# A graph-attention kernel: TensorE gets four unread products at each of its five waits of a slot, and two PSUM banks hold two uses each

## The reference, cut to what matters

```python
x = x + _L0_gnn_ref(_layernorm(x), edge_index, ...)      # attention, 4 heads
x = x + _L0_ffn_ref(_layernorm(x)[None], ...)[0]         # 6 experts, top 2
x = x + _L1_gnn_ref(_layernorm(x), edge_attr_64, ...)    # attention, 1 head
x = x + _L1_ffn_ref(_layernorm(x)[None], ...)[0]         # 8 experts, all
# inside an attention:
e = leaky_relu(a_src[src] + a_dst[dst])
m = segment_max(e, dst); e = exp(e - m[dst])
out = segment_sum(e / segment_sum(e, dst)[dst] * h[src], dst)
```

## Time and profile before

| | us |
|---|---|
| median of 3 runs | 5728.6 |
| lowest and highest | 5703.49 and 5729.56 |
| the profiled execution's own time | 5700.18 |
| its span, first to last instruction | 5698.1 |
| first attention, steady part, 50 slots from 336.1 to 1848.6 | 1512.5, 30.9 a slot |
| second attention, steady part, 50 slots from 2926.2 to 4378.7 | 1452.5, 29.6 a slot |

### The profile page before, as it was taken

The page is one execution under the profiler, slowest core; times in us unless marked ns, Lnnn a source line. Parts: engine busy times, 40 slices in busy tenths (PEclk is TensorE's granted clock), DMA queues, the critical chain, the costliest instruction groups (busy, mean ns, idle before and its releaser), DMA issues. The chain is left out here.

```text
span 5698.1 us, 88959 instructions
## 1 busy us (share of the span) xinstructions
PE 4033.3 (71%) x21808; PEld 3026.7 (53%) x21809; DVE 2571.1 (45%) x8219; ACT 1553.1 (27%) x4325; POOL 2144.2 (38%) x2095
## 2 busy tenths in 40 slices
PE   5176666676667777884356666666666699999999
PEld 3144444444444456773234444444444488888888
DVE  7255555555555677555333343333433451222111
ACT  2122222222222221331222222222222233333333
POOL 0455555555555402327555555555555200000000
PEclk9565666655665556996666666666666699999999
DMA  3222222222222322443333333323223400000000
GB/s 98 70 73 69 70 71 70 72 68 70 71 68 72 53 85 80 163 141 102 91 74 75 73 71 72 72 72 74 71 70 71 81 6 7 5 5 5 5 5 8
DMA packets 382428, 367.94 MB, mean 65 GB/s; under 512 B 249324, under 2 KB 309388, under 8 KB 382242
## 3 DMA queue, kind: packets, MB, share of 16 engines
q0 software_dynamic: 107072, 272.84, 18.7%
q1 hardware_dynamic: 272774, 92.39, 6.7%
q10 hardware_dynamic: 2396, 0.84, 0.1%
HBM read 324.13 MB, written 41.59 MB: 64 GB/s over the span
## 5 line engine op out<-in xcount | busy, mean ns | idle before, releaser
L681 POOL DMA_INDIRECT g_G<-rows,g_pack x1856 | 1895.8, 1021 | 1793.9 <-PE bank L714 1105.5
L714 PE MATMUL bank<-g_G,g_MB 128*125 128x260 f32 x1856 | 833.7, 616 | 418.8 <-DVE acc L921 379.7
L714 PE MATMUL bank<-g_G,g_M 128*125 128x257 f32 x1856 | 760.5, 572 | 419.6 <-DVE acc L921 404.0
L714 PEld LDWEIGHTS bank<-g_G,g_MB 128*125 128x125 f32 x1856 | 529.8, 304 | 639.7 <-DVE acc L921 362.9
L714 PEld LDWEIGHTS bank<-g_G,g_M 128*125 128x125 f32 x1856 | 497.1, 285 | 608.5 <-DVE acc L921 414.4
L921 DVE SCALAR_TENSOR_TENSOR acc<-acc,g_c,bank 125x65 f32 (+1 forms) x2320 | 623.9, 319 | 220.3 <-PE bank L714 150.7
L1363 DVE SCALAR_TENSOR_TENSOR X<-bank,e_cw,X 125x256 f32 (+1 forms) x400 | 175.2, 480 | 844.9 <-PE bank L1189 844.9
L1259 ACT ACTIVATE e_h<-bank,e_bi_c,e_sc_c 128x250 f32<-128x250 f32 x800 | 403.6, 555 | 559.4 <-PE bank L1180 421.6
L1023 DVE TENSOR_SCALAR g_gone<-bank 125x64 f32<-125x64 f32 (+1 forms) x116 | 23.2, 200 | 1129.6 <-remote 1076.6
L787 ACT ACTIVATE g_mt_d<-bank,unode 125x256 bf16<-125x256 f32 x928 | 384.1, 464 | 521.0 <-PE bank L699 492.4
L863 ACT ACTIVATE g_c<-g_delta 125x32 f32<-125x32 f32 (+1 forms) x116 | 25.4, 219 | 1592.1 <-DVE g_delta L1061 1534.1
(11 more groups left out here) (300 smaller groups left out, 4608.4 us busy)
## 6 DMA issues: line engine op xcount, KB each, us to landing
g_G<-rows,g_pack POOLq DMA_INDIRECT x1856
acc<-in_edge_attr SPq DMA_DIRECT2D x50, 531.2 KB
g_pack<-edge_pack SPq DMA_DIRECT2D x928, 2.0 KB
g_drow<-edge_dst SPq DMA_DIRECT2D x928, 1.0 KB
expert_out<-x_y SPq DMA_DIRECT2D x54, 256.0 KB
g_qe<-edge_q SPq DMA_DIRECT2D x464, 1.0 KB
rows<-acc SPq DMA_DIRECT2D x25, 253.9 KB
rows<-n_T SPq DMA_DIRECT2D x25, 251.0 KB
```

The source lines that it names most:

```text
L681: nc.gpsimd.indirect_dma_start(G[:, r, q, :], None, rows_d[l], bass.IndirectOffsetOnAxis(ap=pack[:, r, q, 0:1], axis=0)).then_inc(S(p + f" ...
L714: mm_ = nc.tensor.matmul(bank[4 + u % 2][0:TN, 0:HW], left, G[:, rk, q, :], start=(c == 0), stop=(c == C - 1))
```

## The change

`busy()` issues four bf16 products of 128 x 128 by 128 x 512 into bank 7. Their operands are the constant table `iota_b`, and nothing reads their result. It has no wait and counts up nothing. It is called ahead of five waits in TensorE's order: ahead of the row turn, ahead of the selection turn, ahead of `sums(2, 0)`, ahead of the products for the maxima, and ahead of those at L766. To make bank 7 free, `selT_ps` moves into bank 0 beside `rowT_ps`, and `Xe_ps` moves into bank 6 beside `V_ps`. No wait or count of a semaphore changes.

```diff
+WARM = 4
...
-            selT_ps = bank[1][:, 0:2 * QH]
+            selT_ps = bank[0][:, 2 * P:2 * P + 2 * QH]
...
-            Xe_ps = bank[7][:, 0:KM * QH]
+            Xe_ps = bank[6][:, 2 * P:2 * P + KM * QH]
...
+                    def busy():
+
+                        for _ in range(WARM):
+                            nc.tensor.matmul(bank[7][:, :], iota_b[:, :], iota_b[:, :].unsqueeze(1).broadcast_to([P, 4, P]), start=True, stop=True)
+
                     def slot(i, r, t):
...
+                        busy()
                         if one:
                             if l == 0:
                                 pe.wait_ge(S(p + f"rows_in{r1}"), filled(t, r, 1, 16 * Q))
...
                         sums(3, U - 1)
+                        busy()
                         if one:
 
                             pe.wait_ge(S(p + "SEL"), i)
...
+                        busy()
                         sums(2, 0)
                         sums(2, 1)
...
                         sums(2, 3)
+                        busy()
                         if one:
 
                             pe.wait_ge(S(p + "MB"), i * V)
...
                         sums(2, 5)
+                        busy()
                         if one:
 
                             pe.wait_ge(S(p + "rhs"), i)
```

## The result

The changed kernel takes 5866.1 us (median of 4 runs, 5847.0 to 5879.0), the one before 5716.2 us beside it (4 runs, 5703.5 to 5729.6). The ratio is 1.026, with an interval of 1.024 to 1.029: slower by 150 us. The forecast, 5873, was 7 us off. As will be seen, that is in part luck: two terms of its sum were wrong in opposite directions.

The account below looks back on a forecast made before the run. GpSimd's gathers and its two waits were taken to set the slot. Over 58 slots each, 2.0 us (first attention) and 0.5 (second) gave 116 + 29 = 145; 5700.18 + 145 = 5845, plus 28 to the median: 5873, range 5640 to 6080.

Parts of the forecast that it names:

- Call 1: Ahead of the row turn, wholly in wait A and on the path: adds 1.7 us a slot at the low clock.
- wait A: GpSimd's idle 3.09 us a slot, ended by `sums(3, 6)`; said to grow to 4.5 to 5 us.
- wait B: GpSimd's idle 6.10 us a slot, until VectorE's L1023 and `sums(2, 4)`; expected to change by nothing.
- Calls 2 and 3: Around the selection turn, where a gather has no reserve: 0.7 us a slot, ends -0.6 and +2.9.
- Calls 4 and 5: Ahead of L754 and L766: up to 1.7 us each, hidden by 3.8 us of cover and 2.58 us idle; nothing.
- The credit for the clock in the second attention: A higher clock shortens the second attention's slot: 1.2 us credited beyond call 1's 1.7, leaving +0.5 a slot.
- 1.6 us after the last gather: In the first attention, L1023 starts 1.6 us after GpSimd's last gather, though V's products were recorded as ended earlier.
- if wait A doesn't grow: Sign of being wrong: it would mean that the clock was already up when call 1 began.
- the clock pays: Rival: high clock from call 1 on, slots 1.3 and 1.9 us shorter, 5543 us; 0.23 together with a between case, 5671.
- It cancels: Rival: the second attention gains what the first loses, 5700 to 5757 us; chance 0.13.
- the clock doesn't rise: Rival: every call paid at the low clock, 4.6 us a slot in both attentions, 6263 us; chance 0.09.
- More small costs: Rival: 40 more instructions a slot hold up L754 or L766 during the gathers, 6071 us; chance 0.1.

Follow-up runs that it names:

- e2: Kernel before with the two tiles moved and only call 1, ahead of the row turn: 5764.2 us, ratio 1.007.
- e3: Kernel before with the two tiles moved and only calls 4 and 5, ahead of L754 and L766: 5724.6 us, ratio 1.002.
- e7: The whole change, but each call only in slots that have units to select for: 5827.0 us, ratio 1.021 to the kernel before.
- e4: Kernel before with the two tiles moved and only calls 2 and 3, ahead of the selection turn and `sums(2, 0)`: 5816.9 us, ratio 1.018.
- e10: Kernel before, no calls, the 32 products that make V issued twice at their old place, so 64: 5872.9 us, ratio 1.030.
- e6: None of the five calls; twelve unread products in each slot behind the products of V instead: 5710.5 us, ratio 0.999 to the kernel before.
- e5: Kernel before, no unread products, V's 32 products moved up to stand behind `sums(2, 1)`: 5425.2 us, ratio 0.949.
- e12: Kernel before with V made by 16 products behind `sums(2, 1)`, plus the whole change, on another chip: 4759.0 us against 4784.3, ratio 0.995.

## Why the prediction came out, step by step

- **The price of an unread product**: nearly right. Four take 1.9 us with overlap at the low clock and 1.02 at the high one, against 1.7 and 0.9.
- **Call 1**: the step that failed. I put it wholly on the path at the low clock: 1.7, less 0.4, times 116 is 151 us. e2 gives 53, and in the change wait A grows by 0.4 and 0.6 us a slot instead of 1.3. In the first attention the clock is up when call 1 begins in 32 of 50 slots, and in 25 it holds to the end of `sums(3, 6)`, which gives back what the call takes. In the second, call 1 mostly runs at the low clock still (30 of 50), and only `sums(3, 6)` is faster in part of the slots. Call 5 ahead of L777 has its share in this: in e2, without it, call 1 takes under 1.3 us in none of the 50 steady slots of either attention. The earlier trace rows spoke of a clock that products of call 5 hadn't touched; I priced calls one by one where they act on each other. In e2, where call 1 was alone, wait A did grow by 1.7 and 1.9 us, and wait B gave back 1.7 and 1.5. This second half of the failed step is the fixed wait B, below; why V comes sooner in e2 no run shows.
- **Calls 2 and 3**: the mechanism was right, a gather without reserve behind `sums(2, 0)`; the size was 0.9 instead of 0.7, 106 us instead of 81. In the profile of the change the gather behind them waits 0.5 us longer in the first attention and 1.4 in the second.
- **Calls 4 and 5**: forecast as nothing, and 13 us in e3.
- **The banks**: nothing, as forecast.
- **The credit for the clock in the second attention**, 1.5 us a slot less than in the first, 87 us: wrong. Its clock rose from 0.63 to 0.77 and its slots from 29.6 to 31.0 us. Two slots in the earlier trace rows had differed in clock and length, and I read the one as the cause of the other. More slots would not have warned me: in the kernel before, the 25 of 50 with the higher clock (0.67) are 29.0 us long and the others (0.60) 30.2. Only the run with the clock raised shows that the higher clock doesn't make them short.
- **The edges**: left out of the sum, some 30 us by e7. They are contained in what e2, e3 and e4 cost.
- **"1.6 us after the last gather"**: still so in the change (45 and 50 of 50 slots, 1.6 and 1.7 us in the middle one), and yet no rule: 3.4 us in e10, and `gone` inside the run in 21 of 50 slots of e2's first attention. It let me call 6 us of wait fixed that moving V removes. Of "because of the gathers, not because of TensorE" only the first half stands: `V` itself goes up late, and it does so by the number and the place of TensorE's small products among the gathers.

The sum: 53 + 106 + 13 - 5 for the banks is 167, with 150 measured. Mine, 151 + 81 - 87 = 145, came near because the credit of 87 us, which was not there, ate up most of the 98 that call 1 had been charged too much. That is luck. Of what I had said the profile would show, the clock above 0.7 came true. The first attention's slot (31.4, not 32 to 33), wait A (3.5, not 4.5 to 5) and the second's slot (31.0, not 29.5 to 30.5) did not. Of the two signs of being wrong, "if wait A doesn't grow" came true in half the slots of the first attention. "If the wait of L1023 shrinks" came true there in part (445.8 to 408.7 us), and `gone` started inside the run of gathers in 5 of 50 slots.

Among the rivals, "the clock pays" is out: it forecast 1.3 us less a slot in the first attention once the clock is up from call 1 on, and the 25 slots where that is so are as long as before. Even eight products in each call, with the clock at 0.86, only add to the time. "It cancels" (5700 to 5757) and "the clock doesn't rise" (6263) are out by the 5866 and by the clock of 0.76. The granted clock did follow the added products (0.61 to 0.76, 0.86 with eight). The Trainium skill's rule cited with that rival ("TensorE: Matmul & The Clock Gate", Part 1) is borne out so far, but the slots waited for something else. "More small costs" is partly there: rests of TensorE for "issue" exist, but e3's 13 us show that products ahead of L764 and L777 hardly make them worse.

## What to carry to other kernels

A higher clock on an engine is worth only the part of its work that something waits for; products that keep it up cost their own time wherever the next consumer has no reserve, and what idle time hid here (e6) did not keep the clock up until it ended. Calls that act on a shared state, as the clock is, can't be priced one by one. A long wait with a constant offset to some other engine's work is worth one experiment that moves the late producer, before it is taken as fixed: here that gave 5%, where the change itself cost 2.6%. And when such a wait is removed, look where it went: here, in the second attention, of the 5.0 us that wait B lost, 2.4 came back in wait A, behind the next group of small products, and 1.7 ahead of unit 2.

## What the runs showed of the hardware

- While GpSimd issues gathers without rest, a dense group of small products on TensorE can be drawn out by rests for which the profile shows no wait. V's 64 products took 9.0 and 10.2 us with 3.4 and 4.5 us of rests (e10), and the 48 of L766 took 7.0 us with 4.9 us of rests in e5's second attention. Placing V's group nearer the start of the run, or halving it, freed V, but the rests then stood in L766. In e12, on another chip, L778 had none.
- The semaphore of such a group can go up long after the recorded end of its last product: 5.3 and 6.5 us on the mean for V in the kernel before, with the consumer starting 0.02 us behind the semaphore. In the waits this shows as "remote".
- One of the four chips of the experiments ran the unchanged kernel in 4784 us instead of 5704 to 5716. In e12, the one profile from it, the stages outside the attentions take as long as elsewhere. Ratios from different chips can't be compared for this kernel.
- The clock was up when twelve unread products began and was at 0.50 from 1017.0 on, 2.2 us behind their recorded end at 1014.83 (e6).
